# Selective scan on one core: the sum over states as three 32-column matmuls side by side

## The chip, the cores and the metric

One core of one Trainium2 chip. The time is the device time of one execution in microseconds. The kernel before took 18508.96 us (median of three runs, 18503.32 to 18516.95).

## The reference

Two layers on 32 images of 96 channels, 48 x 48 pixels (L = 2304 positions). Layer 0 is a selective state-space model over the pixels sorted by similarity, with a depthwise convolution before and beside it, and a small FFN; layer 1 is a deformable convolution and a second FFN. The change lies in the scan of layer 0:

```python
def step(hst, t):
    dt_l, B_l, C_l, x_l = t
    dA = jnp.exp(dt_l[..., None] * A)
    hst = dA * hst + (dt_l * x_l)[..., None] * B_l[:, :, None, :]
    y = jnp.einsum('bkdn,bkn->bkd', hst, C_l)
    return (hst, y)
```

There are K = 2 directions, D = 96 channels and N = 16 states per channel. The last line, a sum over the 16 states of state times C, is what the change computes in another form.

## The kernel before, in words

The kernel has two passes over the images. Pass one (`pass_one`, roughly the first 60% of the span) does layer 0's convolution, sort and scan; pass two does the rest. Pass one is a software pipeline: each call (a stage) normalises and convolves image n, orders image n-1, scans image n-2 and finishes image n-3. A stage has 72 steps (`STEPS`), and every engine runs the same loop over `s`, each with its own part of the step, in program order; semaphores tie them.

The 2304 positions are cut into three spans of 768 (`SC`), and two directions make six rounds `q`. A round has 12 steps (`ROUND`): four groups of states (`ng`) by three groups of 32 channels (`cg`). One step handles 32 channels x 4 states, the 128 partitions: partition 32 j + i is channel i of the group and state 4 j + ng. In step s:

- TensorE `replicate(s)` (line 699, bf16) spreads B over the partitions into one of two PSUM areas; the areas go round among steps and the occasional jobs dt, bc, back, eback and seq, and each waits for the user two places before it (`wait_free`).
- DVE `drives(s)` (line 1055) multiplies by dt times x, and `recurrence(s)` (line 1071) scans along the 768 positions into `h[s % 4]`. The scan waits for GpSimd's product of step s-4.
- ScalarE `decays(s)` (line 893) makes the decay for it, and `keep` (line 901) saves the last column for the next span.
- GpSimd (POOL, line 1271) multiplies `h` by the replicated C (`crep`, fetched by SyncE) into `hc[s % HC]`. It waits until TensorE has added what the buffer held: with HC = 4, state s-4.
- TensorE `add_state(s - 3)` (line 710, fp32, `LAG` = 3), right behind `replicate(s)`, sums the 4 states of each channel. Its weights `sel[:, cg, :]` are 128 x 96 with ones only in the 32 columns of the step's channel group, and all 12 steps of a round accumulate into one 96 x 768 area (`BY`). DVE's `take_sum` (lines 1082 and 1086) reads it at the end of the round.

```python
m = pe.matmul(wide(BY, C)[:, a:b], Wt["sel"][:, cg, :], hc[:, v % HC, a:b],
              start=(v % ROUND == 0), stop=(v % ROUND == ROUND - 1))
```

Behind these TensorE has, in the same step, `order` (transposes and rank counts), `local_conv` (line 790, two taps a step until step 35) and `normalise` (lines 725 and 729 from step 46, three taps of line 740 from step 52 to 69). POOL has, beside the products, the softplus parts of dt, two indirect gathers a step from step 5 to 13 (line 1259) and two indirect scatters a step from step 46 to 54 (line 1241). DVE has rounding, remainders of B (`rest`, line 1045), the ordering's comparisons and part of the normalisation. `rest` is written once per round, at the steps `BC_AT` = (3, 16, 27, 38, 51, 63). `eout` holds two of the three output pieces that ScalarE turns out at the steps `E_BACK` = (22, 23, 24) (line 1001) and stores a step later (line 995).

Between two stages all semaphores are cleared behind a barrier.

Of the kernel before, what the change touches and what calls it, by code (L numbers as in the profile page):

```python
# [6 lines left out]
BF16 = mybir.dt.bfloat16  # L7
# [10 lines left out]
CH = 8 * W  # L18
# [18 lines left out]
def shape_constants():  # L37

    c = {}
    c["ident"] = np.eye(P, dtype=np.float32)  # L40
    c["centring"] = (np.eye(C) - 1.0 / C).astype(np.float32)
    c["mean"] = np.full((C, C), 1.0 / C, np.float32)
    c["ones"] = np.ones((P, P), np.float32)
    j, i = np.meshgrid(np.arange(P), np.arange(P), indexing="ij")
    c["before"] = (j < i).astype(np.float32)
    r = np.arange(C)
    state = np.repeat(np.arange(N).reshape(NG, NG), GS, axis=1)
    c["pick"] = (r[:, None, None] % (2 * N) == state[None]).astype(np.float32).reshape(C, NG * P)
    c["sel"] = (np.arange(P)[:, None, None] % GS + GS * np.arange(CG)[None, :, None] == r[None, None, :]).astype(
        np.float32).reshape(P, CG * C)  # L50
    c["sel_off"] = (r[:, None] % GS == np.arange(3 * TAPS)[None, :]).astype(np.float32)
    c["shifts"] = np.concatenate([(r[:, None] == r[None, :] + k - 2).astype(np.float32) for k in range(5)], axis=1)
    px = np.arange(P)[:, None, None] + P * np.arange(NT)[None, :, None]
    tap = np.arange(TAPS)[None, None, :]
    c["base_y"] = (px // W - 1 + tap // 3).astype(np.float32).reshape(P, NT * TAPS)
    c["base_x"] = (px % W - 1 + tap % 3).astype(np.float32).reshape(P, NT * TAPS)
    c["border"] = np.ones((1, PH, PW), np.float32)
    c["border"][:, 0] = c["border"][:, -1] = 0
    c["border"][:, :, 0] = c["border"][:, :, -1] = 0
    c["border"] = c["border"].reshape(1, PH * PW)  # L60
    return c
# [11 lines left out]
def build_program(nc, I, out, B=IMAGES):  # L73

    with ExitStack() as top:
# [40 lines left out]
        w_dt = first("w_dt", [C, K, C])  # L116
        w_bc = first("w_bc", [C, K, C])
        pick = first("pick", [C, NG, P], BF16)
        sel = first("sel", [P, CG, C])
        w_conv = first("w_conv", [C + 1, TAPS, C])  # L120
        w_local = first("w_local", [C, TAPS, C])
        a_neg = first("a_neg", [P, K, NG, CG])
# [304 lines left out]
GS = C // CG  # L427
ROUND = NG * CG
STEPS = Q * ROUND
HC = 4  # L430
CRING = 3
LAG = 3
HR = 4
# [23 lines left out]
def pass_one_memory(sbt, ctx):  # L457
# [1 line left out]
    return dict(  # L459
        x=b("x_in", [C, L]), xn=b("xnp", [P, PH, PW]), xpad=b("xcp", [C, PH, PW]), sim=b("sim", [P, L]),  # L460
        rows=b("rows", [P, NT + 1, C]), unit=b("unit", [P, NT + 1, C]), cmp=b("cmp", [P, 2, L], BF16),
        tie=b("tie", [P, 2, P], BF16), one=b("one", [P, 1], BF16), work=b("work", [C, 3, CH]), local=b("local_c", [C, 2, CH]), eout=b("eout", [C, SC]),
        zpart=b("zpart", [C, NCH]), rlen=b("rlen", [P, NT + 1]), flag=b("flag", [P, NT + 1]), dist=b("dist", [P, NT]),
        not_after=b("not_after", [P, NT]), var_y=b("var_y", [P, NT]),
        inv_y=b("inv_y", [P, NT]), sq_y=b("sq_y", [P, NT]), root_y=b("root_y", [P, NT]),
# [8 lines left out]
def pass_one(nc, ps, S, M, Wt, dram, e_image, s_image, o_image, n_image):  # L474
# [9 lines left out]
    col, ident = Wt["col"], Wt["ident"]  # L484
    x, xn, xpad, sim, rows, unit = (M[n] for n in ("x", "xn", "xpad", "sim", "rows", "unit"))
    inv, newton, squares = (M["work"][:, i, :] for i in range(3))
    eout = (M["eout"][:], M["work"][:, 0:2, :].rearrange("p a b -> p (a b)"))
    xs, y, bq, cq, carry = (M[n] for n in ("xs", "y", "bq", "cq", "carry"))

    srows = unit[:, 0:NT, :]  # L490
# [74 lines left out]
    with nc.Block() as block:  # L565
# [78 lines left out]
        def _(pe):  # L644
# [55 lines left out]
                                  start=True, stop=True)  # L700
                m.then_inc(S["s_breps"], 1)

            def add_state(v):

                q, ng, cg = cut(v)
                pe.wait_ge(S["s_weighted"], v + 1)
                if v % ROUND == 0 and q:
                    pe.wait_ge(S["s_y"], q)
                for a, b in pieces:
                    m = pe.matmul(wide(BY, C)[:, a:b], Wt["sel"][:, cg, :], hc[:, v % HC, a:b],  # L710
                                  start=(v % ROUND == 0), stop=(v % ROUND == ROUND - 1))
                m.then_inc(S["s_added"], 1)

            def normalise(s):
# [81 lines left out]
            for s in range(STEPS):  # L796
# [9 lines left out]
                    inputs_of(bc_at[s])  # L806
                if Sc:
                    replicate(s)
                    if s >= LAG:
                        add_state(s - LAG)  # L810
                if O:
                    order(s)
                    local_conv(s)
                if Nx:
                    normalise(s)
            if Sc:
                for v in range(STEPS - LAG, STEPS):
                    add_state(v)

        @block.scalar  # L820
        def _(act):
# [152 lines left out]
            def end(s):  # L974
# [21 lines left out]
                if s in eback_at:  # L996
                    i = eback_at[s]
                    act.wait_ge(S["e_back"], i + 1)
                    if i >= 2:
                        act.wait_ge(S[f"e_saved{i % 2}"], 16 * (i // 2))  # L1000
                    act.activation(eout[i % 2], wide(bank_of(("eback", i)), C), ACT.Identity,
                                   bias=col["n_b"], scale=col["n_g"]).then_inc(S["e_out"], 1)
# [29 lines left out]
        def _(dve):  # L1032
# [6 lines left out]
            def remainder(q):  # L1039
                i = before(q)  # L1040
                dve.wait_ge(S["s_cq"], i + 1)
                dve.wait_ge(S["s_hi"], i + 1)
                if i >= 1:
                    dve.wait_ge(S["s_lo"], i)
                dve.tensor_tensor(rest[:], wide(bank_of(("bc", q)), C), bq[:, q % 2, :],
                                  ALU.subtract).then_inc(S["s_r1"], 1)

# [26 lines left out]

            def take_sum(q):

                dve.wait_ge(S["s_added"], ROUND * (q + 1))
                part = span(q)
                if q < NSC:
                    if E and q == 0:  # L1080
# [133 lines left out]
        def _(pool):  # L1214
# [48 lines left out]
            for s in range(STEPS):  # L1263
                if Sc:
# [2 lines left out]
                        pool.wait_ge(S[f"s_crep{g % CRING}"], 16 * NG * (g // CRING + 1))  # L1267
                    pool.wait_ge(S["s_scanned"], s + 1)
                    if s >= HC:
                        pool.wait_ge(S["s_added"], s - HC + 1)  # L1270
                    pool.tensor_tensor(hc[:, s % HC, :], h[:, s % HR, :], crep[:, g % CRING, :],  # L1271
                                       ALU.mult).then_inc(S["s_weighted"], 1)
                if s - 3 in bc_at:
# [672 lines left out]
```

## Time and profile before

| | |
|---|---|
| median of three runs | 18508.96 us |
| span of the profiled execution, first to last instruction | 18494.4 us |
| median less that span | 14.6 us |
| TensorE (PE) busy | 14302.8 us, 77% |
| VectorE (DVE) busy | 14315.8 us, 77% |
| POOL busy | 12392.9 us, 67% |
| ScalarE (ACT) busy | 9047.7 us, 49% |
| mean granted TensorE clock | 0.803 of full |

Busy shares are averages over both passes. PE is TensorE's matmuls; PEld is its weight loads, which overlap them. In a row of a timeline, the first two numbers are the start and the length in us, then engine, line, operation, output <- input, shapes and count; brackets hold the idle time before it and who ended that. An fp32 matmul of the program shows as two matmul records.

### The profile page before, as it was taken

The page shows a single profiled execution, that of the slowest core. Times are in us where ns is not written, and L with a number is a line of the kernel's source. Part 1 is how long each engine was busy: PE and PEld are TensorE (multiplying, and loading weights), DVE is VectorE, ACT ScalarE, POOL GpSimd, SP SyncE. Part 2 cuts the span into 40 slices and gives each one's busy share as a digit, 9 for nine tenths or more (in the row PEclk, how much of TensorE's full clock was granted, in tenths as well). Part 3 has the DMA queues.
Part 4 walks back from the last instruction along what each step waited for, and adds up shares of the span by engine and source line. Part 5 has one row for each costly group of instructions (what it writes and reads, how often), then busy time and mean ns, then how long its engine had stood idle before and what let it go on. Part 6 is the DMA issues. An engine that isn't in the chain of part 4 may idle for free. (4 is left out here: it accounts for less than half of the span.)

```text
span 18494.4 us, 181487 instructions
## 1 busy us (share of the span) xinstructions
PE 14302.8 (77%) x51055; PEld 6774.5 (37%) x51055; DVE 14315.8 (77%) x17465; ACT 9047.7 (49%) x16414; POOL 12392.9 (67%) x9604
## 2 busy tenths in 40 slices
PE   7877878778778787787877747877777777787776
PEld 3333333334333333333333313333333333333333
DVE  5788788887887878878878746777777777777776
ACT  4555555555555555555555534444444444444443
POOL 3666666666666666666666636777777777777777
PEclk8888888889888898888888866667666766766776
DMA  2333333333333333333333335556565656555654
GB/s 59 90 91 94 88 88 91 93 89 88 94 91 89 90 89 94 90 87 93 88 92 91 89 81 160 172 168 175 167 174 168 174 168 174 169 173 168 174 168 143
DMA packets 1294631, 2228.80 MB, mean 121 GB/s; under 512 B 712841, under 2 KB 756125, under 8 KB 1281629
## 3 DMA queue, kind: packets, MB, share of 16 engines
q1 hardware_dynamic: 893022, 1086.35, 22.7%
q0 software_dynamic: 368640, 1076.24, 20.0%
q10 hardware_dynamic: 32256, 56.64, 1.0%
q8 instruction: 454, 7.44, 0.2%
q14 instruction: 259, 2.12, 0.0%
HBM read 1493.27 MB, written 271.92 MB: 95 GB/s over the span
## 5 line engine op out<-in xcount | busy, mean ns | idle before, releaser
L1497 POOL DMA_INDIRECT G<-corners,idx x5184 | 5615.5, 1083 | 1939.4 <-issue 1653.3
L1271 POOL TENSOR_TENSOR hc<-h,crep 128x768 f32<-128x768 f32 x2304 | 4177.4, 1814 | 3623.7 <-DVE h L1071 2235.0
L710 PE MATMUL ps<-hc,sel 128*96 128x512 f32 (+1 forms) x9216 | 3922.9, 554 | 624.3 <-POOL hc L1271 476.5
L1055 DVE TENSOR_TENSOR ps<-dxr,ps 128x768 f32<-128x768 f32 x2304 | 2186.8, 949 | 1497.0 <-PE ps L699 1492.1
L1071 DVE TENSOR_TENSOR_SCAN h<-decay,carry,ps 128x768 f32<-128x768 f32 x1536 | 2776.5, 1808 | 207.0 <-ACT decay L893 147.0
L1788 DVE TENSOR_TENSOR G<-G,ps 128x1536 f32<-128x1536 f32 (+1 forms) x1152 | 2239.5, 1945 | 612.6 <-DMA G<-corners,idx 612.4
L710 PEld LDWEIGHTS ps<-hc,sel 128*96 128x96 f32 x9216 | 1539.7, 182 | 2568.7 <-issue 1756.5
L893 ACT ACTIVATE decay<-dtr,a_neg 128x768 f32<-128x768 f32 x2304 | 2120.1, 926 | 262.1 <-DVE h L1071 242.0
L699 PE MATMUL ps<-bq,pick 96*128 96x512 bf16 (+1 forms) x4608 | 1272.7, 361 | 1214.9 <-DVE h L1071 907.6
L1798 DVE TENSOR_TENSOR G<-G 128x384 f32<-128x384 f32 (+1 forms) x3456 | 1967.2, 600 | 27.6
L790 PE MATMUL ps<-xcp,w_local 96*96 96x384 f32 x3456 | 1511.7, 561 | 3.3 <-ACT local_c L965 1.4
L1515 PE MATMUL ps<-ident,G 128*96 128x128 f32 x5184 | 1221.3, 363 | 329.9 <-PEq L162 179.8
L1528 PE MATMUL ps<-cols_t,w_def 96*96 96x384 f32 x3456 | 1309.0, 539 | 181.3 <-ACT prow L1716 174.8
L1071 DVE TENSOR_TENSOR_SCAN h<-decay,ps 128x768 f32<-128x768 f32 x768 | 1341.1, 1746 | 60.1 <-ACT decay L893 34.2
L901 ACT ACTIVATE carry<-h 128x1 f32<-128x1 f32 x1536 | 304.0, 198 | 2097.3 <-DVE h L1071 2088.1
L1671 ACT ACTIVATE sq<-ps 96x384 f32<-96x384 f32 x576 | 280.5, 487 | 2119.3 <-PE ps L1535 2119.3
L740 PE MATMUL ps<-xnp,w_conv 97*96 97x384 f32 x3456 | 1229.3, 492 | 4.7 <-ACT x_in L930 2.5
L1515 PEld LDWEIGHTS ps<-ident,G 128*96 128x96 f32 x5184 | 852.6, 171 | 932.5 <-DVE G L1798 420.6
L699 PEld LDWEIGHTS ps<-bq,pick 96*128 96x128 bf16 x4608 | 388.2, 104 | 2000.5 <-DVE h L1071 1138.9
L1665 ACT ACTIVATE cols_t<-ps 96x512 f32<-96x512 f32 (+1 forms) x1728 | 828.1, 480 | 340.4 <-PE ps L1515 336.5
L1528 PEld LDWEIGHTS ps<-cols_t,w_def 96*96 96x96 f32 x3456 | 609.2, 181 | 816.9 <-issue 583.2
L1542 PE MATMUL ps<-sq,mean 96*96 96x384 f32 x1152 | 766.9, 761 | 137.0 <-ACT sq L1671 118.1
(216 smaller groups left out, 21667.7 us busy)
## 6 DMA issues: line engine op xcount, KB each, us to landing
crep<-c_rows SPq DMA_DIRECT2D x3072, 96.0 KB, 2.2
dtr<-rel SPq DMA_DIRECT2D x2304, 96.0 KB, 2.1
dxr<-mag SPq DMA_DIRECT2D x2304, 96.0 KB, 2.2
corners<-prow SPq DMA_DIRECT2D x1536, 72.0 KB
G<-corners,idx POOLq DMA_INDIRECT x5184
x_in<-in_x SPq DMA_DIRECT2D x32, 864.0 KB, 6.3
local_all<-local_c ACTq DMA_DIRECT2D x192, 144.0 KB, 2.4
sim<-sorted_rows SPq DMA_DIRECT2D x32, 864.0 KB, 5.9
```

The source lines that it names most:

```text
L699: m = pe.matmul(wide(bank_of(("step", s)), P)[:, a:b], Wt["pick"][:, ng, :], bq[:, q % 2, a:b], start=True, stop=True)
L710: m = pe.matmul(wide(BY, C)[:, a:b], Wt["sel"][:, cg, :], hc[:, v % HC, a:b], start=(v % ROUND == 0), stop=(v % ROUND == ROUND - 1))
L790: m = pe.matmul(ps[0:C, BV, 0:CH], Wt["w_local"][:, t, :], xpad[:, 8 * c + t // 3:8 * c + t // 3 + 8, t % 3:t % 3 + W], start=(t == 0), st ...
L893: act.activation(decay[:, s % 3, :], dtr[:, q % 2, cg, :], ACT.Exp, scale=Wt["a_neg"][:, direction(q)[0], ng, cg:cg + 1]).then_inc(S["s_de ...
L1055: dve.tensor_tensor(drive, dxr[:, q % 2, cg, :], drive, ALU.mult).then_inc(S["s_drive"], 1)
L1071: dve.tensor_tensor_scan(along(h[:, v % HR, :], k), along(decay[:, v % 3, :], k), along(wide(bank_of(("step", v)), P), k), first, ALU.mult ...
L1271: pool.tensor_tensor(hc[:, s % HC, :], h[:, s % HR, :], crep[:, g % CRING, :], ALU.mult).then_inc(S["s_weighted"], 1)
L1497: pool.indirect_dma_start(M["G"][:, slot(g), k, :], None, dram["tables"][side(r)], bass.IndirectOffsetOnAxis(M["idx"][side(r)][:, t, k:k + ...
L1515: m = pe.transpose(ps[0:C, BT + n % 2, (k % 4) * P:(k % 4 + 1) * P], M["G"][:, slot(t - 1), k, 0:C], ident[:])
L1528: m = pe.matmul(ps[0:C, BN, 0:CH], Wt["w_def"][:, k, :], M["cols"][:, of_e(w)[1] % 2, k, :], start=(k == 0), stop=(k == TAPS - 1))
L1788: dve.tensor_tensor(rows, rows, by.to_broadcast([P, (k1 - k0) * CORNERS, C]), ALU.mult).then_inc(S["p_mul"], 1)
L1798: dve.tensor_tensor(rows[:, :, 0:C], rows[:, :, 0:C], rows[:, :, q * C:(q + 1) * C], ALU.add).then_inc(S["p_half" if q < CORNERS - 1 else ...
```

## The change

The sums of three steps (one `ng`, the three channel groups) are issued together, once every third step. `sel` is now one 128 x 32 matrix for all groups, and each step's sum is written to its own 32 partitions of the area, by its own 32 columns of the array. `s_added` counts groups of three. GpSimd has five product buffers instead of four. `eout`'s first buffer is dropped and `rest` is used in its place, with two waits for that.

```diff
-    c["sel"] = (np.arange(P)[:, None, None] % GS + GS * np.arange(CG)[None, :, None] == r[None, None, :]).astype(
-        np.float32).reshape(P, CG * C)
+    c["sel"] = (np.arange(P)[:, None] % GS == np.arange(GS)[None, :]).astype(np.float32)
...
-        sel = first("sel", [P, CG, C])
+        sel = first("sel", [P, GS])
...
-HC = 4
+HC = 5
...
-        ... local=b("local_c", [C, 2, CH]), eout=b("eout", [C, SC]),
+        ... local=b("local_c", [C, 2, CH]),
...
-    eout = (M["eout"][:], M["work"][:, 0:2, :].rearrange("p a b -> p (a b)"))
+    eout = (M["rest"][:], M["work"][:, 0:2, :].rearrange("p a b -> p (a b)"))
...
-            def add_state(v):
-                q, ng, cg = cut(v)
-                pe.wait_ge(S["s_weighted"], v + 1)
-                if v % ROUND == 0 and q:
+            def add_states(g):
+                q, ng = g // NG, g % NG
+                pe.wait_ge(S["s_weighted"], CG * (g + 1))
+                if ng == 0 and q:
                     pe.wait_ge(S["s_y"], q)
                 for a, b in pieces:
-                    m = pe.matmul(wide(BY, C)[:, a:b], Wt["sel"][:, cg, :], hc[:, v % HC, a:b],
-                                  start=(v % ROUND == 0), stop=(v % ROUND == ROUND - 1))
+                    for cg in range(CG):
+                        m = pe.matmul(wide(BY, P)[GS * cg:GS * (cg + 1), a:b], Wt["sel"][:],
+                                      hc[:, (CG * g + cg) % HC, a:b], start=(ng == 0), stop=(ng == NG - 1))
                 m.then_inc(S["s_added"], 1)
...
-                    if s >= LAG:
-                        add_state(s - LAG)
+                    if s >= LAG and (s - LAG) % CG == CG - 1:
+                        add_states((s - LAG) // CG)
...
-                for v in range(STEPS - LAG, STEPS):
-                    add_state(v)
+                for g in range((STEPS - LAG) // CG, STEPS // CG):
+                    add_states(g)
...
                 if s in eback_at:
                     i = eback_at[s]
                     act.wait_ge(S["e_back"], i + 1)
+                    rests = sum(BC_AT[q - 1] < E_BACK[0] for q in rounds)
+                    if i == 0 and rests:
+                        act.wait_ge(S["s_lo"], rests)
...
                     dve.wait_ge(S["s_lo"], i)
+                if E and BC_AT[q - 1] > E_BACK[0]:
+                    dve.wait_ge(S["e_saved0"], 32)
                 dve.tensor_tensor(rest[:], wide(bank_of(("bc", q)), C), bq[:, q % 2, :],
...
-                dve.wait_ge(S["s_added"], ROUND * (q + 1))
+                dve.wait_ge(S["s_added"], NG * (q + 1))
...
                     if s >= HC:
-                        pool.wait_ge(S["s_added"], s - HC + 1)
+                        pool.wait_ge(S["s_added"], (s - HC) // CG + 1)
```

## Rows read from the trace of the kernel before

**Rows 1.** The page, costliest groups and DMA issues of the whole span.
```profile
L1271 POOL TENSOR_TENSOR hc<-h,crep 128x768 f32<-128x768 f32 x2304 | 4177.4, 1814 | 3623.7 <-DVE h L1071 2235.0
...
local_all<-local_c ACTq DMA_DIRECT2D x192, 144.0 KB, 2.4
```

**Rows 2.** Windows of one stage: stretch, length, busy (count) by engine, clock, DMA.
```profile
4924.60:5259.10 334.50, 266.60 (x1001) 128.87 (x1001) 273.71 (x264) 180.72 (x287) 211.96 (x138) 0.89 0.35 90
...
5195.27:5247.55 52.28, 50.53 (x189) 26.65 (x188) 38.81 (x38) 38.52 (x52) 30.97 (x21) 1.00 0.28 68
5145.40:5195.27 49.87, 41.10 (x130) 19.19 (x131) 37.50 (x41) 29.22 (x52) 45.17 (x34) 0.93 0.39 101
4955.30:5006.00 50.70, 38.19 (x112) 17.12 (x111) 41.25 (x37) 25.60 (x39) 46.33 (x33) 0.87 0.45 114
5006.00:5064.00 58.00, 45.31 (x205) 22.60 (x204) 52.89 (x45) 35.75 (x67) 29.62 (x17) 0.94 0.36 97
5064.00:5145.40 81.40, 59.31 (x259) 26.43 (x257) 78.69 (x89) 29.93 (x46) 45.53 (x26) 0.79 0.36 90
4924.60:4955.30 30.70, 24.94 (x90) 13.97 (x91) 18.17 (x16) 18.41 (x32) 9.06 (x5) 0.83 0.23 63
5247.55:5259.10 11.55, 7.22 (x22) 2.91 (x20) 6.39 (x5) 3.29 (x4) 5.29 (x4) 1.00 0.35 84
```

**Rows 3.** Waits, 3000 to 8000 us: total us, times, longest us.
```profile
DVE ps L1055 <- PE ps L699: 697.9, 465, 5.7
...
DVE h L1071 <- ACT decay L893: 88.3, 92, 1.6
```

**Rows 4.** Groups by shape, 3000 to 8000 us: busy, mean ns, idle before.
```profile
L710 PE MATMUL ps<-hc,sel 128*96 128x512 f32 x2151 | 1283.9, 682 | 287.9 <-POOL hc L1271 220.9 <-DVE y L1082 65.1 <-DVE y L1086 0.4
...
L710 PE MATMUL ps<-hc,sel 128*96 128x256 f32 x2152 | 728.9, 424 | 0.0
```

**Rows 5.** Timeline near the stage's end, convolution beside the scan.
```profile
5240.43 0.96 DVE L1055 TENSOR_TENSOR ps<-dxr,ps 128x768 f32<-128x768 f32 x1 [0.59 <-PE ps L699]
...
5243.79 1.45 PE L710 MATMUL ps<-hc,sel 128*96 128x512 f32 x4
5243.99 0.96 DVE L1055 TENSOR_TENSOR ps<-dxr,ps 128x768 f32<-128x768 f32 x1 [0.69 <-PE ps L699]
5245.04 1.81 DVE L1071 TENSOR_TENSOR_SCAN h<-decay,carry,ps 128x768 f32<-128x768 f32 x1
5245.08 2.10 PE L740 MATMUL ps<-xnp,w_conv 97*96 97x384 f32 x6
...
5247.02 0.49 PE L699 MATMUL ps<-bq,pick 96*128 96x512 bf16 x2
...
5250.07 1.81 DVE L1071 TENSOR_TENSOR_SCAN h<-decay,carry,ps 128x768 f32<-128x768 f32 x1 [1.56 <-ACT decay L893]
```

**Rows 6.** TensorE's timeline in pass two, line 1616 beside line 1535.
```profile
14028.33 1.50 PE L1616 MATMUL ps<-xn,w_off 96*32 96x384 f32 x6
14029.87 1.59 PE L1535 MATMUL ps<-x,centring 96*96 96x384 f32 x2
14031.39 1.50 PE L1616 MATMUL ps<-xn,w_off 96*32 96x384 f32 x6
...
14164.35 0.85 PE L1616 MATMUL ps<-xn,w_off 96*32 96x384 f32 x6
```

**Rows 7.** Timeline in the first stretch in which POOL is full.
```profile
4982.59 1.86 PE L710 MATMUL ps<-hc,sel 128*96 128x512 f32 x4 [2.26 <-POOL hc L1271]
...
4987.53 0.96 DVE L1055 TENSOR_TENSOR ps<-dxr,ps 128x768 f32<-128x768 f32 x1 [4.23 <-PE ps L699]
```

**Rows 8.** Timeline, the last sum of a stage.
```profile
5256.58 1.53 PE L710 MATMUL ps<-hc,sel 128*96 128x512 f32 x4 [1.23 <-POOL hc L1271]
```

**Rows 9.** Timeline, the store of `eout` and the next use of `rest`.
```profile
5042.53 0.32 ACTq L995 DMA_DIRECT2D mamba_all<-eout x1
...
5052.40 0.94 DVE L1045 TENSOR_TENSOR rest<-ps,bq 96x768 f32<-96x768 f32 x1
```

More of the change, by code:

```diff
@@ L461, in pass_one_memory @@
         rows=b("rows", [P, NT + 1, C]), unit=b("unit", [P, NT + 1, C]), cmp=b("cmp", [P, 2, L], BF16),
-        tie=b("tie", [P, 2, P], BF16), one=b("one", [P, 1], BF16), work=b("work", [C, 3, CH]), local=b("local_c", [C, 2, CH]), eout=b("eout", [C, SC]),
+        tie=b("tie", [P, 2, P], BF16), one=b("one", [P, 1], BF16), work=b("work", [C, 3, CH]), local=b("local_c", [C, 2, CH]),
         zpart=b("zpart", [C, NCH]), rlen=b("rlen", [P, NT + 1]), flag=b("flag", [P, NT + 1]), dist=b("dist", [P, NT]),
```

## The prediction

> **What bounds the kernel now.** I read the page first, for the busy shares of the whole and how often the step of pass one runs [rows 1]; then a table of one repetition of pass one's loop body (a stage, 334.5 us) cut into seven stretches [rows 2]; then the totals of waits over fifteen stages [rows 3]; then the order of instructions inside the stretches where the waits sit.
>
> Products: 2304 in all [rows 1], one a step, 72 a stage, so 32 stages carry a scan. The change touches only these, some 10,600 us of the span.
>
> VectorE (DVE) carries the recurrence: a drive (0.96 us) and a scan (1.81 us) per step. In the stage of [rows 2] it is busy 273.7 of 334.5 us, so 60.8 us are idle, and almost all of this idle time has one releaser: the drive waits for TensorE's replication of B, 697.9 us over 15 stages, 46.5 us a stage, against 5.9 us a stage for ScalarE's decay [rows 3]. The reader should see in [rows 2] that this is not one regime but five:
> - First 30.7 us and last 11.6 us: start and end of the stage, latency.
> - Two stretches in which GpSimd (POOL) is full, 46.3 of 50.7 us and 45.2 of 49.9 us: product, two indirect DMAs, product, two indirect DMAs. DVE idles there too, 9.5 and 12.4 us, but TensorE is not what is missing.
> - Two in the middle, 58 and 81.4 us, in which DVE is 91% and 97% busy.
> - 52.3 us near the end: TensorE busy 50.5, at the full clock (1.00, so 2.4 GHz), DVE 38.8, ScalarE 38.5. Here TensorE is the bound.
>
> In this last stretch [rows 5] show why. TensorE works in program order: the sum matmuls of one state begin at 5243.79, the three taps of the convolution at 5245.08, the next replication at 5247.02. So the sums hold the engine for 1.29 us, the taps for 1.94 us, and the drive comes 0.69 us late in a step of 3.56 us. The sums are the largest TensorE group of pass one: 1283.9 + 728.9 us over 5000 us [rows 4].
>
> **The change, part by part.**
>
> *The sums.* Before: four matmul records per state (two column pieces, two fp32 passes each), 1.29 us at full clock; three states 3.87 us. After: still twelve records per three states, but each with 32 weight columns and an own 32-partition output. The price rests on whether three of them run side by side. Pass two has this form already: line 1616, three outputs at 32-partition offsets in one bank, different moving data. Six records of 384 columns took 0.85 us at full clock and 1.50 us at half [rows 6]; directly behind, two full-width records of 384 columns took 1.59 us at half clock. So six narrow records cost what two wide ones do: three run together. Twelve then cost what four do, 1.29 us per group of three states: 2.58 us less TensorE time per group, at full clock.
>
> *Switching between narrow and wide.* At half clock two passes of 384 fp32 columns stream in about 1.28 us (line 1616's back-to-back records repeat so), while line 1535 starts 1.54 us after line 1616, and line 1616 again 1.52 us after line 1535 [rows 6]: at most 0.26 and 0.24 us around each switch, some of it perhaps ordinary. I charge 0.5 us a group, bounds 0 and 0.5. Net 2.1 us per group.
> The Trainium skill (TensorEngine Tiling (Array Packing), Key Properties) says that a change of tiling mode drains the engine; the trace allows for that only the half microsecond already charged. It (TensorE: Matmul & The Clock Gate, Part 3) also gives 2.38 times for three column tiles of 512: by that, an estimate, a group would take 3.87/2.38 = 1.63 us before switches, so about 0.3 us more than by the trace, or 1.5 us a stage in the bound stretch.
>
> *The bound stretch (52.3 us, 13 steps, 4.33 groups).* TensorE 50.5 - 4.33 x 2.1 = 41.4 us. DVE needs 38.8, ScalarE 38.5. What is late next: six replications in this stretch share a PSUM bank with dt, B/C, rows-back or sequence work and cannot start before the previous scan ends; that costs DVE 0.59 us each [rows 5], 3.5 us. ScalarE's silu waits for the taps and the decay behind it makes the scan wait 1.56 us every third or sixth step [rows 5]; with earlier taps I keep 1.2 us in all. 38.8 + 3.5 + 1.2 = 43.5; three engines near 39 to 41 us never mesh fully, so 44. Gain 8.3 us; bounds 4 and 10.
>
> *The first POOL stretch.* POOL's own work stays, so its length stays. But the 4.23 us DVE wait arises because the sums waited for a product, took 1.86 us and had convolution behind them [rows 7]. Now TensorE stands behind POOL only at every third step, and DVE leaves the stretch further ahead. Gain 2 us, bounds 0 and 4.
>
> *The second POOL stretch.* Same, but its largest waits go over the low part of B, which POOL itself delivers. Gain 1 us, bounds 0 and 3.
>
> *The middle stretches.* DVE idle 5.1 and 2.7 us, part of it bank sharing. Gain 1.8 us, bounds 0 and 3.
>
> *The first 30.7 us.* DVE idles 12.5 us, but sums start only at step 3 (now 5). 0.
>
> *The end.* Before, the last state's four records wait for the last product and then take 1.53 us [rows 8]. Now TensorE has nothing between the group of states 66 to 68 and that product, idle some 7 us, and the twelve records may run at half clock, 2.9 instead of 1.5. Loss 1.3 us, bounds 0 and 1.5 (DVE and all behind it wait).
>
> *Clock.* In the table the granted clock follows TensorE's busy share: 97% goes with 1.00, 82% with 0.93, 78% with 0.94, 73% with 0.79 [rows 2]. The sums drop by some 24 x 2.1 = 50 us of 267 a stage, so outside the bound stretch the share falls to about 60% and more matmuls run at 1.2 GHz. Most of that lies beside POOL or DVE; I charge 1.5 us, bounds 0 and 12.
>
> *Five product buffers.* POOL's product s now waits for the group of state s-5 instead of state s-4. That group goes out at TensorE's step 3g+5, behind the replication of the same step; POOL needs it only for product 3g+5, which comes after a drive and a scan (2.77 us), longer than 1.29. When POOL is behind, it has two products (3.6 us) to do first. So nothing; if TensorE stood late by more than that, POOL would wait, at most 1 us a group. DVE's reuse of its state ring is unchanged.
>
> *eout in rest.* The remainder for round 3 now waits for the store of the third output. That store is issued at 5042.53, and the remainder starts at 5052.40 [rows 9]: 9.9 us, against 2.4 us to landing for stores of half that size [rows 1]. Nothing; at DVE it would hold the scan behind it. The wait on ScalarE is for its own earlier work. The smaller weight load at the start: nothing.
>
> **Sum.** 8.3 + 2 + 1 + 1.8 - 1.3 - 1.5 = 10.3 us a stage, x 32 = 330 us. The span of 18494.4 lies 14.6 us under the median of 18508.96, a difference that I leave as it is: 18494.4 + 14.6 - 330 = 18180 us.
>
> **Rivals.**
> 1. *DVE rules everywhere.* The groups free TensorE so far that only POOL and bank sharing hold DVE, and the upper bounds hold together: 10 + 4 + 3 + 3 = 20 us a stage, 640 us, 17870. For it: 46 us of waits per stage name TensorE. Against it: POOL is above 90% busy in two stretches, and ScalarE is close behind at the end.
> 2. *Cold TensorE, slower.* With the sums gone, TensorE's share in the middle stretches falls below what keeps its clock; at 1.2 GHz a step there costs replication 0.7, two local taps 3.0 (two pairs of records of 1.5 us [rows 6]), a third of a group 0.9 and ordering some 0.4, about 5 us against DVE's 3.2. If a third of the 58 us stretch and the two POOL stretches (38 steps) ran so and cost 1.5 us each, that is 19 us, against 10 gained: 9 x 32 = 290, 18800. It decides once the clock cost passes 12 us a stage. For it: clock 0.79 at 73%. Against: in exactly that stretch DVE idled only 2.7 us of 81, and an engine that falls behind becomes busy again. The skill (TensorE: Matmul & The Clock Gate, Part 1) says idle stretches halve the clock; the trace agrees with that direction.
> 3. *No concurrency here.* High and low passes alternate on the same columns, and in-order starts allow no overlap: a group takes 3.87 us and blocks the next replication in one lump. In the bound stretch nothing changes, elsewhere lumps outlast the lead of one step: 0 to 3 us a stage, 18510 to 18600. Against: line 1616 has the same alternation.
> 4. *Hidden anyway.* ScalarE and bank sharing take the place of TensorE: 3 us in the bound stretch, the rest eaten by clock and end: under 1 us a stage, 18480 to 18540.
>
> **How the numbers follow.** Forecast (100 to 500 us gained) 0.67, rival 1 0.13, rival 2 0.08, rival 3 0.04, rival 4 0.08. Runs of the kernel differ by 14 us, so 0.2% (37 us) is what can be told from no change. Faster: 0.67 + 0.13 + a little of rival 4 = 0.82; same 0.08; slower 0.10. Range 17850 to 18460: the sum of lower bounds (4 us - 1.5 - 1) to rival 1.
>
> **What would show it.** Line 710's twelve matmul records in about 1.3 to 1.8 us at full clock, starting three at a time; if 3.9 us, rival 3. In the stretch before the stage's end, steps of about 3.2 us instead of 4.0, and DVE waits for line 699 mostly of 0.59 us. POOL stretches still 50 us. Waits of the drive for TensorE down from 46 to about 30 us a stage. Clock of pass one between 0.7 and 0.85. It is wrong if DVE's wait for line 699 stays with short groups (clock, rival 2), or if it moves to the decay (ScalarE, rival 4).

## The result, and the profile after

The changed kernel takes 18551.83 us (median of 10 runs, 18511.81 to 18591.22), the kernel before 18514.15 us (10 runs, 18500.47 to 18519.77) on the same chip. The ratio is 1.0021, 95% interval 1.0013 to 1.0030. The forecast was 18180 us, a gain of 1.8%; the gain did not come at all.

The profiled execution took 18591.22 us, the slowest of the ten and 39 us over their median (1.2 us a stage, if it all lay there), with a span of 18589.4 us, 95 us over the span before. Pass one's last sum is read by VectorE at 10938.4 us, before at 10868.5: 70 of the 95 us lie in pass one. The other 25 us lie in pass two, which the change doesn't touch, and I can't attribute them.

Three readings show what happened. First the windows of one stage, in order of time. The inner cuts lie at the drives of steps 6, 17, 29, 47, 58 and 70, in the kernel before within 2 us of the cuts of [rows 2]; the columns are the same (stretch, length, busy time with count for PE, PEld, DVE, ACT and POOL, granted clock, DMA share, GB/s). The last row is the whole stage.

```profile
4952.17:4982.95 30.78, 22.87 (x87) 12.07 (x88) 18.01 (x15) 18.39 (x31) 9.06 (x5) 0.75 0.21 63
4982.95:5035.14 52.19, 30.74 (x122) 11.22 (x120) 45.78 (x40) 26.74 (x40) 45.88 (x33) 0.78 0.46 116
5035.14:5090.86 55.72, 41.34 (x194) 17.93 (x194) 49.97 (x43) 33.62 (x64) 28.55 (x16) 0.71 0.36 96
5090.86:5173.69 82.83, 53.40 (x257) 17.55 (x260) 79.59 (x91) 30.85 (x46) 46.63 (x26) 0.56 0.35 88
5173.69:5223.76 50.07, 39.37 (x136) 15.50 (x131) 37.94 (x42) 29.14 (x52) 45.24 (x34) 0.77 0.40 101
5223.76:5277.79 54.03, 48.38 (x188) 21.95 (x187) 39.59 (x37) 39.01 (x53) 31.14 (x20) 0.87 0.28 69
5277.79:5290.10 12.31, 4.70 (x26) 1.09 (x26) 6.37 (x6) 2.79 (x3) 5.88 (x4) 0.80 0.28 65
...
4952.20:5290.10 337.90, 240.79 (x1001) 97.30 (x1001) 277.25 (x263) 180.54 (x287) 212.38 (x138) 0.73 0.35 90
```

Between the same drives the stage before [rows 2] took 30.55, 52.64, 54.95, 82.52, 50.00, 52.28 and 11.55 us. The stretch that TensorE bounds is 54.03 us long now, 1.75 more. TensorE is still busy for 48.4 of it although the sums need a third of their time: the clock there fell from 1.00 to 0.87, and over the whole stage from 0.89 to 0.73. The other six moved by less than 1 us each.

Second, the drive's waits from 3000 to 8000 us (total us, times, longest us), beside [rows 3]:

```profile
DVE ps L1060 <- PE ps L698: 640.8, 443, 6.1
...
DVE h L1076 <- ACT decay L893: 58.4, 84, 1.3
```

The waits for the replication fell from 697.9 to 640.8 us, that is from 46.5 to 42.7 us a stage where I expected some 30. The wait for the decay did not grow: ScalarE has not taken TensorE's place.

Third, TensorE's costliest groups in the same 5000 us (busy us, mean ns of one | idle time before), beside [rows 4]:

```profile
L790 PE MATMUL ps<-xcp,w_local 96*96 96x384 f32 x1575 | 788.6, 630 | 0.3
L740 PE MATMUL ps<-xnp,w_conv 97*96 97x384 f32 x1620 | 667.3, 554 | 6.5 <-ACT x_in L930 6.5
L710 PE MATMUL ps<-hc,sel 128*32 128x512 f32 x2136 | 550.0, 859 | 231.6 <-POOL hc L1276 231.6
L698 PE MATMUL ps<-bq,pick 96*128 96x512 bf16 x1066 | 515.8, 484 | 715.0 <-DVE h L1076 487.8 <-DVE rest L1050 96.1 <-PEq L161 80.6
L698 PE MATMUL ps<-bq,pick 96*128 96x256 bf16 x1066 | 358.5, 336 | 0.0
L710 PE MATMUL ps<-hc,sel 128*32 128x256 f32 x2136 | 305.9, 517 | 0.0
```

The sums (line 710) went from 1283.9 + 728.9 to 550.0 + 305.9 us, less than half. Everything beside them became longer, though its code is unchanged. In the kernel before, a record of the local convolution (line 790) took 561 ns, one of the convolution (line 740) 490, one of the replication (512 columns) 424. Now they take 630, 554 and 484 ns.

The timeline of TensorE and DVE at the end of this stage, answering to [rows 5] and [rows 8], shows both prices:

```profile
5250.42 1.80 DVE L1076 TENSOR_TENSOR_SCAN h<-decay,carry,ps 128x768 f32<-128x768 f32 x1
5252.28 0.82 PE L698 MATMUL ps<-bq,pick 96*128 96x512 bf16 x2 [2.53 <-DVE h L1076]
5252.90 4.05 PE L740 MATMUL ps<-xnp,w_conv 97*96 97x384 f32 x6
5256.73 0.85 PE L698 MATMUL ps<-bq,pick 96*128 96x512 bf16 x2
5257.51 2.78 PE L710 MATMUL ps<-hc,sel 128*32 128x512 f32 x12
...
5263.95 0.96 DVE L1060 TENSOR_TENSOR ps<-dxr,ps 128x768 f32<-128x768 f32 x1 [3.46 <-PE ps L698]
...
5271.05 1.49 PE L710 MATMUL ps<-hc,sel 128*32 128x512 f32 x12
5272.47 2.18 PE L740 MATMUL ps<-xnp,w_conv 97*96 97x384 f32 x6
...
5286.31 2.78 PE L710 MATMUL ps<-hc,sel 128*32 128x512 f32 x12 [6.46 <-POOL hc L1276]
5289.15 0.95 DVE L1091 TENSOR_TENSOR y<-y,ps 96x768 f32<-96x768 f32 x1 [4.78 <-PE ps L710]
```

Twelve narrow records take 1.49 us at 2.4 GHz (the next matmul starts 1.42 us behind their start), so three groups do run side by side. At 1.2 GHz they take 2.78 us. TensorE waited 2.53 us for the scan at 5252.28, because this replication shares a bank with the scan before it. The records behind that idle time are slow: the six convolution records take 4.05 us against 2.10 in [rows 5], the group behind them 2.78, and two drives later DVE stands for 3.46 us. The saved time had become idle time in front of TensorE's next work, and that work ran at half clock.

### The profile page after: what moved, and what is told of

It reads as the page before. It is cut to its first block and busy times, and to the rows that moved or that the text cites. A ratio compares the mean times of both kernels' runs of the same rounds, so it can differ in the third digit from the quotient of the medians.

```text
span 18589.4 us, 181609 instructions
## 1 busy us (share of the span) xinstructions
PE 13442.4 (72%) x51055; PEld 5756.8 (31%) x51055; DVE 14426.8 (78%) x17465; ACT 9034.6 (49%) x16414; POOL 12433.5 (67%) x9604
## 5 line engine op out<-in xcount | busy, mean ns | idle before, releaser
L698 PE MATMUL ps<-bq,pick 96*128 96x512 bf16 (+1 forms) x4608 | 1472.4, 412 | 1593.0 <-DVE h L1076 1086.6
L710 PE MATMUL ps<-hc,sel 128*32 128x512 f32 (+1 forms) x9216 | 1711.9, 695 | 515.2 <-POOL hc L1276 515.2
L790 PE MATMUL ps<-xcp,w_local 96*96 96x384 f32 x3456 | 1724.3, 628 | 2.3 <-ACT local_c L965 1.4
L1533 PE MATMUL ps<-cols_t,w_def 96*96 96x384 f32 x3456 | 1348.6, 552 | 179.8 <-ACT prow L1721 172.9
L740 PE MATMUL ps<-xnp,w_conv 97*96 97x384 f32 x3456 | 1403.0, 548 | 17.6 <-ACT x_in L930 15.4
L710 PEld LDWEIGHTS ps<-hc,sel 128*32 128x32 f32 x9216 | 384.2, 138 | 1691.8 <-issue 1064.5
```

The lines of the kernel that those rows point to most:

```text
L698: m = pe.matmul(wide(bank_of(("step", s)), P)[:, a:b], Wt["pick"][:, ng, :], bq[:, q % 2, a:b], start=True, stop=True)
L710: m = pe.matmul(wide(BY, P)[GS * cg:GS * (cg + 1), a:b], Wt["sel"][:], hc[:, (CG * g + cg) % HC, a:b], start=(ng == 0), stop=(ng == NG - 1))
L790: m = pe.matmul(ps[0:C, BV, 0:CH], Wt["w_local"][:, t, :], xpad[:, 8 * c + t // 3:8 * c + t // 3 + 8, t % 3:t % 3 + W], start=(t == 0), st ...
L1533: m = pe.matmul(ps[0:C, BN, 0:CH], Wt["w_def"][:, k, :], M["cols"][:, of_e(w)[1] % 2, k, :], start=(k == 0), stop=(k == TAPS - 1))
```

## The experiments

Two theories stood at the start. **A, the clock:** TensorE time that is saved comes back as a lower granted clock, and the other matmuls get longer by what the sums got shorter. **B, the lump:** three states' sums at once block the next replication, whatever the clock. Later kernels asked whether A can be turned to account by filling TensorE's idle time.

The table gives ratio to the kernel before with its 95% interval, the mean lengths of the six rounds (end of one sum's reading by DVE to the next) and of the stage, over 26 stages of each profiled execution, and the granted clock from 5000 to 8000 us. Each row of stages is one execution: those of the changed kernel and of e3 were the slowest of their ten, 39 and 51 us over the median, so differences of 1 to 2 us a stage between rows can be the execution's. On the chips of e1 to e4 and e9 to e14 the kernel before took 19442 to 19494 us; so I compare ratios and the stages of pass one, not times.

| kernel | ratio | r0 | r1 | r2 | r3 | r4 | r5 | stage us | clock |
|---|---|---|---|---|---|---|---|---|---|
| before | 1 | 73.1 | 54.0 | 63.0 | 44.0 | 58.4 | 42.1 | 334.6 | 0.89 |
| changed | 1.0021 (1.0013-1.0030) | 70.7 | 57.1 | 63.4 | 44.7 | 58.2 | 43.0 | 337.1 | 0.73 |
| e7 changed again | 1.0012 (1.0003-1.0022) | 70.3 | 57.3 | 63.4 | 44.5 | 57.5 | 42.5 | 335.4 | 0.75 |
| e1 wide groups | 1.0345 (1.0328-1.0362) | 72.5 | 56.7 | 64.1 | 50.6 | 59.5 | 52.4 | 355.8 | 0.84 |
| e2 narrow each step | 1.0082 (1.0065-1.0099) | 73.5 | 53.9 | 63.1 | 44.0 | 60.4 | 44.7 | 339.6 | 0.89 |
| e3 buffers only | 0.9995 (0.9985-1.0004) | 73.0 | 54.0 | 63.0 | 44.0 | 59.3 | 43.0 | 336.4 | 0.89 |
| e4 filler | 1.0133 (1.0116-1.0150) | 69.2 | 56.4 | 63.2 | 44.0 | 63.7 | 46.4 | 343.0 | 0.81 |
| e5 two pieces | 1.0030 (1.0018-1.0041) | 75.5 | 58.5 | 60.8 | 47.4 | 58.7 | 35.0 | 335.9 | 0.73 |
| e6 filler early | 1.0004 (0.9995-1.0014) | 70.5 | 56.5 | 63.4 | 44.0 | 58.8 | 41.2 | 334.5 | 0.80 |
| e8 third per step | 1.0010 (1.0000-1.0020) | 73.5 | 54.6 | 63.3 | 44.0 | 60.3 | 39.2 | 334.9 | 0.70 |
| e14 no sums | 1.0046 (1.0030-1.0063) | 73.5 | 57.8 | 63.1 | 44.0 | 59.6 | 40.0 | 337.9 | 0.66 |
| e9 warm ends | 0.9988 (0.9979-0.9998) | 70.4 | 56.6 | 63.4 | 44.0 | 58.8 | 41.2 | 334.5 | 0.81 |
| e10 before, warm ends | 1.0023 (1.0013-1.0033) | 74.6 | 53.4 | 63.5 | 43.9 | 58.4 | 42.4 | 336.2 | 0.89 |
| e11 pieces, warm ends | 1.0018 (1.0008-1.0028) | 75.3 | 58.2 | 60.8 | 47.4 | 59.5 | 35.5 | 336.6 | 0.75 |
| e12 filler at waits | 1.0016 (1.0007-1.0026) | 68.8 | 56.4 | 63.3 | 44.0 | 59.7 | 42.6 | 334.8 | 0.81 |
| e13 two at waits | 1.0056 (1.0040-1.0073) | 70.2 | 56.7 | 63.1 | 44.0 | 59.5 | 44.3 | 337.7 | 0.80 |

(e5 and e11 read each sum one step later, which makes r0 longer and r5 shorter by a step.)

**e1, wide groups.** The changed order and buffers, but each state's sum at full width as before:
```diff
-  pe.matmul(wide(BY, P)[GS*cg:GS*(cg+1), a:b], Wt["sel"][:], hc[...], start=(ng == 0), ...)
+  pe.matmul(wide(BY, C)[:, a:b], Wt["sel"][:, cg, :], hc[...], start=(ng == 0 and cg == 0), ...)
```


> The three sums stay grouped every third step, but with the wide weights of before (128 x 96), so a group takes 3.87 us of TensorE at full clock; buffers as in the changed kernel. Theory A (the freed TensorE time lowered its clock, and the colder clock took the gain back): busy time is as before the change, so the clock of pass one goes back to about 0.88 and the time to that of the kernel before or a little above it, 18500 to 18650, the rest being the price of the lump. Theory B (the lump itself costs what narrow columns gain): clearly slower than before, by the 10 us a stage that the change should have gained, 18850 or more.

Measured: 3.5% slower than before, rounds 3 and 5 longer by 6.6 and 10.3 us. A lump of three wide sums does cost: the waits of the drive for replication and of POOL for the sums are

```profile
DVE ps L1061 <- PE ps L699: 733.7, 417, 5.3
...
POOL hc L1277 <- PE ps L711: 243.3, 84, 6.6
```

So narrow columns earn 3.2% against the same order with wide ones, and the grouping alone would have lost that. It doesn't follow that the short lump costs anything; e5 and e8 test that.

**e2, narrow each step.** No groups: each state's sum goes out at its own step as before, but in its 32 columns:
```diff
+  pe.matmul(wide(BY, P)[GS*cg:GS*(cg+1), a:b], Wt["sel"][:], hc[:, v % HC, a:b], ...)   # state v alone
```


> Narrow sums (128 x 32 weights), one state per step as before, so nothing runs side by side: TensorE streams the same 1.29 us a step as before, no lumps. Theory A in the form that only busy time counts for the clock: clock of pass one 0.88, time 18500 +- 40. Theory A in the form that the number of active columns counts: clock falls to 0.75 or less with TensorE's work undiminished, 18700 to 19200. Theory B: as before, 18500.

Measured: ratio 1.0082 with the same clock as before:

```profile
5000.00:8000.00 3000.00, 2466.95 (x8853) 909.39 (x8852) 2427.31 (x2338) 1596.48 (x2548) 1881.29 (x1224) 0.89 0.35 90
```

So the narrow columns alone did not lower the clock here. They do cost something, most likely at each switch: TensorE is busy 2467 us here against 2393 before in the same window. The loss of 0.82% (about 160 us in 2304 steps, 70 ns a step) is what my bound of 0.5 us for a group's switches allowed.

**e3, buffers only.** The kernel before, with `HC = 5` and the third output kept in `rest`, with its two waits.

> The sums of before, one wide state per step, with the five product buffers and with eout's first piece in rest and its two waits. Theory C (these parts cost the missing gain): 18600 to 18850. Theories A and B: within 30 us of before, 18490 to 18540.

Measured: 0.9995, no difference, as the prediction had it. What effect the change has lies in the sums.

**e4 and e6, fillers.** A matmul of no use is put where a step has no sum; it writes the fourth 32 partitions of the bank. e4 does so at every such step, e6 only in steps before 48, so that the convolution stretch has none:
```diff
+  def keep_busy():
+      pe.matmul(wide(BY, P)[C:P, 0:512], Wt["sel"][0:C, :], Wt["w_conv"][0:C]...[:, 0:512], ...)
   if s >= LAG and (s - LAG) % CG == CG - 1: add_states(...)
+  elif s >= LAG: keep_busy()          # e4
+  elif LAG <= s < 48: keep_busy()     # e6
```


> The changed kernel with one matmul more in each of the two steps of three that have no group: 32 columns x 512, constant data, into the unused partitions 96 to 127 of the sum's bank, no waits, 0.85 us at full clock. Theory A: the clock of pass one rises from 0.73 towards 0.85 and the stage shortens although TensorE has more to do, 18300 to 18450. Theory B: more work, no gain, 18550 to 18750. If active columns count for the clock and not busy time, the clock stays near 0.73 and the time rises to 18600 or more.

> The changed kernel with the filler matmul of e4 (32 columns x 512, constant data, unused partitions) only in steps 3 to 47, not beside the convolution. Theory A: the clock of the first four rounds rises, the rounds 0 and 1 (127.8 us together in the changed kernel, 127.1 before, 125.7 with the filler everywhere) keep the 2 us gained and rounds 4 and 5 stay as in the changed kernel: stage 335, ratio about 1.000. Theory B: nothing to gain there, ratio as the changed kernel or 0.002 above it.

Measured, windows of e4 and then of e6:

```profile
5000.00:8000.00 3000.00, 2419.71 (x9588) 851.79 (x9590) 2425.50 (x2307) 1572.56 (x2499) 1845.91 (x1200) 0.81 0.35 88
```

```profile
5000.00:8000.00 3000.00, 2355.15 (x9514) 871.36 (x9511) 2481.29 (x2361) 1621.79 (x2575) 1902.04 (x1235) 0.80 0.35 91
```

Both raise the clock from 0.73 to 0.8. e4's rounds 4 and 5, which hold 16 fillers, are 8.9 us longer than the changed kernel's: TensorE is on the path there, still. Theory A had expected e4 to be faster than before. e6 costs nothing and wins back at most 2.6 us a stage; against e7 on the same chip the intervals overlap (1.0004 and 1.0012). A higher clock outside the convolution stretch is worth next to nothing.

**e5, two pieces, and e7, the changed kernel again.** e5 sends a group's first half at step 3g+5 and its second at 3g+6, so that the lump is half as long. e7 is a repetition, for the spread from chip to chip.

> The changed kernel with the narrow group of three cut in two pieces of 384 columns, in two of three steps (0.64 us of TensorE each instead of 1.29 once; five buffers; each round's sum is read one step later). Same TensorE work, more even. Theory B (a replication can run ahead of VectorE by at most a step, so the fullest step counts and a lump undoes what the other two steps save): the stage of 337 us falls to 330 or less, ratio 0.985 to 0.993 to before. Theory A (the colder clock alone): no better than the changed kernel, 1.000 to 1.006.

> The changed kernel once more, on the chip of this group of runs, as the base for the others. All theories: ratio 1.002 to before, 1.000 to 1.005.

Measured: e5 1.0030, not better than e7's 1.0012, at the clock of the changed kernel. Halving the lump gains nothing, which speaks against B.

**e8 and e14, the sums left out.** One narrow sum a step with only a third of the columns (0:256), and in e14 with only 4. These two leave out two thirds and practically all of the sum over states; all waits and the order of the kernel before stay. (At the first step of a stage both also fill the area once with a wide matmul, which no other kernel has.)
```diff
+  pe.matmul(wide(BY, P)[GS*cg:GS*(cg+1), 0:256], Wt["sel"][:], hc[:, v % HC, 0:256], ...)   # e8
+  pe.matmul(wide(BY, P)[GS*cg:GS*(cg+1), 0:4], Wt["sel"][:], hc[:, v % HC, 0:4], ...)       # e14
```


> Narrow sums of one state in every step, but only columns 0 to 255 of 768 (the other columns of the sum are left out, so the output differs): a third of the streaming, 0.43 us a step, perfectly even, nothing side by side, no group. The same TensorE time as the changed kernel without its lump. Theory B: the stage falls by some 10 us, ratio 0.975 to 0.985. Theory A: the clock falls to 0.73 as in the changed kernel and the time stays within 0.3% of before.

> Narrow sums of one state a step over 4 columns only: practically all of the sum's streaming is left out (the output differs), with its semaphores and waits kept. It bounds what any saving in the sums can give. Theory A: the clock of pass one falls below 0.70 and the stage stays between 331 and 335 us, ratio 0.990 to 1.001. If only the form of the group had failed: stage 320 to 326, ratio 0.97 or less.

Measured: 1.0010 and 1.0046. This is the decisive pair. With no lump, and with the largest TensorE group of pass one down from 2013 to 267 us in 5000, the stage is no shorter than before; e14's, 337.9 us, is even above the 331 to 335 us that theory A expected. e14's windows, first the long one and then its convolution stretch, again from the drive of step 58 to that of step 70:

```profile
5000.00:8000.00 3000.00, 2040.36 (x7641) 913.37 (x7641) 2463.27 (x2346) 1602.25 (x2545) 1894.05 (x1231) 0.66 0.35 89
...
5233.13:5285.48 52.35, 46.98 (x168) 22.94 (x168) 39.16 (x37) 39.42 (x53) 30.67 (x20) 0.86 0.26 63
```

The stretch is as long as before, 52.35 us, and TensorE is busy for 46.98 of it at clock 0.86, where it was busy for 50.53 at 1.00. Twelve sums of 1.29 us have left it, each leaving 0.2 to 0.3 us, and only 3.6 us less are busy. e14's groups from 3000 to 8000 us say where the rest is:

```profile
L791 PE MATMUL ps<-xcp,w_local 96*96 96x384 f32 x1575 | 941.4, 736 | 0.0
...
L741 PE MATMUL ps<-xnp,w_conv 97*96 97x384 f32 x1620 | 738.1, 602 | 4.2 <-ACT x_in L931 4.2
...
L698 PE MATMUL ps<-bq,pick 96*128 96x512 bf16 x1065 | 559.7, 526 | 653.2 <-DVE h L1077 430.7 <-PEq L161 96.4 <-DVE rest L1051 72.1
```

The same three shapes went from 561, 490 and 424 ns before to 630, 554 and 484 in the changed kernel and 736, 602 and 526 here, with clocks 0.89, 0.73 and 0.66. The timeline around the head of e14's stretch shows it in single instructions:

```profile
5227.34 0.82 PE L698 MATMUL ps<-bq,pick 96*128 96x512 bf16 x2 [2.58 <-ACT unit L878]
5228.09 0.27 PE L711 MATMUL ps<-hc,sel 128*32 128x4 f32 x2
5228.20 0.96 DVE L1061 TENSOR_TENSOR ps<-dxr,ps 128x768 f32<-128x768 f32 x1 [3.44 <-issue]
5228.29 4.16 PE L741 MATMUL ps<-xnp,w_conv 97*96 97x384 f32 x6
...
5233.13 0.96 DVE L1061 TENSOR_TENSOR ps<-dxr,ps 128x768 f32<-128x768 f32 x1 [0.58 <-PE ps L698]
5234.61 3.32 PE L741 MATMUL ps<-xnp,w_conv 97*96 97x384 f32 x6
...
5242.23 2.18 PE L741 MATMUL ps<-xnp,w_conv 97*96 97x384 f32 x6
```

The stretch is entered at 1.2 GHz, behind 2.58 us in which TensorE idled; the first taps take 4.16 and 3.32 us, and only after some 10 us are they back at 2.1. The two slow sets alone cost 2.06 + 1.22 = 3.3 us. The two steps from 5228.20 to 5238.29 take 10.1 us, before 7.9.

**e9, e10, e11, warm ends.** e9 is e6 with four fillers ahead of the last group, which waits for POOL, and two behind it; e10 puts fillers behind the last three sums of the kernel before; e11 is e5 with the fillers of e6 and of e9.

> e6 (the changed kernel with the filler matmul in steps 3 to 47) with four fillers more before the last group of a stage, where TensorE waits over 6 us for the last product, and two behind it, before the barrier. Nothing on the path is added. Theory A (TensorE's clock is what holds the stage): the last group runs in 1.5 us instead of 2.8 and the first matmuls of the next stage run faster, the stage falls from 334.5 by 2 to 6 us, ratio 0.989 to 0.997. If the clock is no more than a companion: 1.000 to 1.002.

> The kernel before with wide sums, only with four fillers (32 columns x 512, unused partitions) around the last sums of a stage. Theory A: the first matmuls of the next stage are faster here too, the stage falls by 1 to 4 us, ratio 0.993 to 0.998, and the gain is the clock's, not the narrow sums'. Otherwise 1.000 to 1.003.

> e5 (group in two pieces in two steps) with the filler in those steps before 48 that have no piece and with the fillers of e9 around the end of the stage. Theory A: e5's evenness can pay once the clock is kept, stage 328 to 332, ratio 0.985 to 0.993. Without an effect of the clock: 1.003 as e5.

Measured: 0.9988, 1.0023, 1.0018. Only e9 is faster than before, by 0.12%, interval 0.02 to 0.21%. Its rounds are e6's to 0.1 us and its stage is that of the kernel before, so the fillers at the end did not earn it, and what did is not shown. Its timeline shows why they did nothing: the first of them ran beside the narrow group before, as a fourth 32-column part, and all were done 4.29 us before the last product came.

```profile
5244.66 0.63 PE L715 MATMUL ps<-hc,sel 128*32 128x512 f32 x3
5244.70 0.62 PE L704 MATMUL ps<-w_conv,sel 96*32 96x512 f32 x1
5246.01 2.31 PE L704 MATMUL ps<-w_conv,sel 96*32 96x512 f32 x5
...
5252.62 1.08 PE L715 MATMUL ps<-hc,sel 128*32 128x512 f32 x3 [4.29 <-POOL hc L1287]
```

The last group still starts after 4.29 us of idleness, at 1.2 GHz: three records of 512 columns take 1.08 us there, 0.63 us ahead of the fillers. e9 as a whole is the best version measured, by less than the 0.2% that the prediction called the least one can tell. What theory A expected of the warm ends (ratios of 0.985 to 0.998) came in none of the three.

**e12 and e13, fillers at the waits.** e6, with one filler (e12) or two (e13) ahead of each replication in the convolution stretch that must wait for the previous step's scan.
```diff
+  if s >= 50 and order_of_use[use[("step", s)] - 2] == ("step", s - 1): keep_busy()   # e13: twice
```


> e6 plus one filler (32 columns x 512, 0.85 us at full clock) directly ahead of the replication in the eight steps from 50 on in which it waits for the previous step's scan (51, 56, 60, 61, 63, 64, 66, 68), where TensorE stands idle. Theory A (cold stretches behind these idle times hold rounds 4 and 5): rounds 4 and 5, 100.0 us in e6, fall by 1 to 4 us, ratio 0.988 to 0.998 to before. If TensorE's work and not its clock is the limit there: they rise by 1 to 5 us, 1.003 to 1.015.

> As e12 with two fillers at each of the eight places (1.7 us at full clock), so that idle times of 2 us and more are filled too. Theory A: rounds 4 and 5 as in e12 or 1 to 3 us better where the idle time is long. Otherwise worse than e12 by as much again.

Measured: 1.0016 and 1.0056; rounds 4 and 5 are 2.3 and 3.8 us longer than in e6, where theory A expected them shorter. Here the filler comes into time that looks idle (2.53 us in the timeline above), and it still costs more than the warmth gives back.

## Why the prediction was wrong

**The step that failed is the bound stretch.** It was to give 8.3 us of the 10.3, by "TensorE 50.5 - 4.33 x 2.1 = 41.4 us", all at the full clock; and of the clock the prediction said "Most of that lies beside POOL or DVE; I charge 1.5 us, bounds 0 and 12". Both halves are wrong. Over 26 stages the stretch took 52.9 us on average in the changed kernel, before 52.3. The changed kernel's own stages tell the two halves apart, because they differ among themselves. With the same instructions the stretch took 54.03 us at clock 0.87 (the row above), and in three other stages:

```profile
6237.49:6289.89 52.40, 46.75 (x188) 21.54 (x187) 39.58 (x37) 39.01 (x53) 31.17 (x20) 0.90 0.28 68
6575.02:6625.52 50.50, 44.85 (x190) 21.17 (x189) 39.49 (x36) 39.56 (x53) 31.12 (x20) 0.96 0.28 67
6910.08:6959.69 49.61, 43.95 (x188) 20.65 (x187) 39.48 (x38) 39.01 (x53) 31.13 (x20) 0.97 0.30 71
```

None of the 26 ran it at 1.00 throughout, but e8, whose sums take about the same time of TensorE, did in some stages. Here are one of those and the next stage:

```profile
6200.07:6248.66 48.59, 44.82 (x167) 20.63 (x167) 38.96 (x37) 39.35 (x53) 31.02 (x20) 1.00 0.27 66
6532.13:6583.34 51.21, 47.44 (x167) 21.54 (x168) 39.07 (x37) 39.06 (x52) 30.46 (x20) 0.95 0.24 58
```

So at the full clock short sums are worth 3.7 us here (52.28 less 48.59), not 8.3, and a clock of 0.97 to 0.87 takes 1.0 to 5.4 us back, which at 0.87 is more than was saved. TensorE's 41.4 us were measured as 44.8 at the full clock and 48.4 at 0.87. (e8's stages with such a stretch take 328 to 332 us, but most of them follow one of 336 us or more, and its mean is 334.9: the saving did not last.)

Why only 3.7 at the full clock: some steps do not depend on the sums at all. Step 60 takes 5.01 us before, in e8 and in e14. VectorE works for 4.35 us of it, and then waits 0.66 us for a replication that could not start before the scan in its bank had ended. Step 63 takes 6.13 us before and in e8, and step 67 4.94. The prediction had counted such waits as 3.5 + 1.2 us. How the clock takes the rest back is plainest with no sums. The steps 59 to 62 and then 63 to 65, before and in e14:

```profile
5198.66:5218.04 19.38, 19.38 (x69) 9.94 (x68) 14.20 (x16) 15.93 (x24) 9.96 (x7) 1.00 0.09 26
5218.04:5231.94 13.90, 12.15 (x49) 6.58 (x48) 10.85 (x13) 9.82 (x12) 6.65 (x6) 1.00 0.10 32
...
5238.29:5255.83 17.54, 15.78 (x62) 7.78 (x61) 14.74 (x15) 15.73 (x23) 9.01 (x7) 1.00 0.07 22
5255.83:5272.41 16.58, 14.05 (x44) 6.46 (x43) 10.84 (x13) 9.82 (x12) 8.70 (x7) 0.69 0.10 27
```

In all, the eight steps of this stretch that e14 ran at the full clock took 30.6 us, before 35.0; the four others took 21.7, before 17.3. The gain and the loss are equal, 4.4 us.

Rounds 4 and 5 together took 100.5 us before, 101.2 in the changed kernel, 100.0 in e7, 99.6 with no sums (e14). The prediction also miscounted: the 52.3 us hold 12 drives and four groups, not 13 and 4.33, so a step took 4.4 us and not 4.0. And its range ran from "4 us - 1.5 - 1", with the clock at 1.5 us; with its own bound of 12 the range would have reached beyond no change. The fall of the clock itself it had foreseen ("between 0.7 and 0.85", measured 0.73), though busy share and clock go together in only four rows of [rows 2]: the other three have 75% with 0.87, 81% with 0.83 and 63% with 1.00.

**The first POOL stretch** was to give 2 us and gave 0.3 (mean of 26 stages, drive of step 6 to drive of step 17). VectorE gains 4.3 us in steps 10 to 12 and loses 4.0 in steps 13 to 16. In e6, at clock 0.93 in the latter, it is 3.8 and 3.3, so the clock is not the main reason. POOL's 18 gathers take 42.4 us from the first to the last before, 42.1 in the changed kernel, and at step 16 of the stage from 4276 us on, VectorE waits 0.54 us for the last one's landing. The clause "DVE leaves the stretch further ahead" is what failed. **The second** (1 us) gave nothing, 50.0 and 50.1 us. **The middle** (1.8 us) lost 1.0, 137.5 and 138.5 us, while its clock fell from 0.94 and 0.79 to 0.73 and 0.57.

**The end** (-1.3 us) was right: the last reading waits 4.78 us for twelve records of 2.78, before 3.51 for records of 1.53 [rows 8]. The last drives come closer together, so that the part behind step 70 is only 0.75 us longer.

**The price of a group** (1.29 us, some more with switches) was right: 1.42 to 1.49 us at 2.4 GHz. **Buffers and `eout`** at nothing: right (e3).

**The rivals.** Rival 3 (no concurrency) is refuted by the timeline. Rival 4 came nearest, with 3 us in the bound stretch, "the rest eaten by clock and end", and 18480 to 18540 us, 12 us under the measured time; I had given it 0.08. Its reason holds in part: bank sharing and VectorE's own work keep steps 60 and 63 as they were, with short sums too. But waits for the decay fell, and fillers in the bound stretch (e4, e13) cost time, which they would not if ScalarE or bank sharing alone ruled there. Rival 2 had the mechanism of the rest: at half clock, steps cost more than the sums had saved. It placed it in the middle stretches, where it is small in the changed kernel; in e14 steps 17 to 28 do take 57.7 us at clock 0.68, before 55.0 at 0.94. Against it I had said that "an engine that falls behind becomes busy again". It does, but only after some 10 us (e14), in a stretch of 52.

**What is shown and what isn't.** Shown: taking the sums' time away, in part or nearly in full, does not shorten the stage, while the clock falls and the other matmuls lengthen (changed, e8, e14); in the bound stretch the same instructions take longer the lower the clock (54.03 to 49.61 us), and the saving is worth 3.7 us where it stays full (e8); narrow columns alone leave the clock at 0.89 (e2); buffers and the lump are not the cause (e3, e5, e8). Not shown: what a whole stage would take at the full clock, and how the loss outside the bound stretch divides. In e14 not all of it is the clock's: the rounding instruction on VectorE (`mag <- one_e, mag`, line 1040, six times a stage) takes 1.88 us on average, before 1.59, in all 1.7 us a stage. It takes 0.95 us when POOL has no product at the same time and 2.96 when POOL's covers 1.83 us of it. Pass two's 25 us in the profiled execution stay open too.

## What to carry to other kernels

Price the work that stays on TensorE at the clock that will be granted after the saving, above all behind waits in the stretch where it is the bound. Go through such a stretch step by step and strike out the steps that another engine or a shared bank holds at their length: here they left 3.7 us of 8.3. Before making a part of TensorE's work cheaper, leave it out altogether and time that: here even a sum for nothing would have gained nothing, which one run shows. Fillers raise the clock and cost nothing where another engine rules, but it is worth nothing there; where TensorE rules, they cost more than they give.

## What the runs showed of the hardware

- In many kernels a stage takes one of two lengths: 334.5 us in 25 of 26 stages before and in all of e6 and e9, 337.9 us in about half of the changed kernel's and in all of e14's. e7, the same program as the changed one, takes 334.5 us in its last 12 stages, and e3, with the sums and the clock of before, takes 337.9 in about half of its own. What selects the length is not shown. A change of a few us in one stretch need not show in the stage.
- The VectorE instruction `mag <- one_e, mag` (96x768, both operands in SBUF) takes 0.95 us alone and up to 2.96 us beside a product on POOL (e14).
- Four matmuls with 32 columns each run side by side: in e9 a filler starts 0.04 us after three narrow records and ends with them.
- On some chips the kernel before takes 930 to 980 us more (19442 to 19494 us). In e3 on such a chip pass one's last sum is read at 10917.3 us of 19484.1, so nearly all of the extra time lies in pass two.
